# Products of constants between TensorE's working stretches, and the tokenizer's last normalisation handed over on the chip for two of sixteen pairs

## The chip, the cores and the metric

One core of one Trainium2 chip runs the whole program, a two-layer language-model tower. The metric is the device time of one execution in microseconds; the kernel before is timed three times, and one of its executions is profiled. TensorE is called PE here, VectorE DVE, ScalarE ACT, GpSimd POOL, and SyncE, which only issues DMAs, SP.

## What is computed

The input is 32 sequences of 512 token numbers. Cut to what matters (each `_layernorm` subtracts the mean over the 64 channels and divides by the deviation):

```
h = tok(x)                       # spectrum features, 64 -> 128 -> gelu -> 64
h = h + neighbourhood_attention(_layernorm(h))   # 8 heads, 31 neighbours, step 2
h = h + top2_of_8_experts(_layernorm(h))         # gelu experts
h = h + decayed_linear_attention(_layernorm(h))  # 0.99 ** distance
h = h + soft_experts(_layernorm(h))   # router softmax(mean over the batch), 8 experts,
                                      # three matrix products each
```

The result is 32 x 512 x 64, float32.

## The kernel before, in words

Two sequences form a pair: their 2 x 64 channels lie on the 128 partitions and the 512 positions in the free dimension. `s.h` holds the 16 pairs of the residual stream, `s.z` their normalised form and much scratch. Nearly all matrix products are float32 and show in the trace as two instructions each (passes).

The program is a row of seven blocks: `prepare`, `token_features`, `neighbourhood_attention`, `mixture_of_experts`, `decayed_attention`, `soft_router`, `soft_experts`. Each block gives every engine a program of its own; the engines meet at the end of each block, and none starts the next one before all have ended. Within a block, `unrolled(count, unroll, (lead, stage), ...)` writes out the loop: at each turn it runs the stages in the order listed, each `lead` items ahead. Every engine executes its instructions in order and waits on counting semaphores (`wait_ge`), so the list of stages is the order of work. `done(n)` is the count that says that item n is finished.

**Normalisation between blocks.** The means are folded into the weights. POOL squares each pair of `h` (`square`), PE sums the squares of four pairs at a time (`variance`, L494) into a bank in which the reciprocal deviations of the 32 sequences get 32 rows, and ACT turns the bank into `s.rstd` by a logarithm and an exponential. SP writes that to DRAM (`hop`, L500) and reads each row back broadcast over 64 partitions (`spread`, L512, two DMAs per pair) into one of four buffers `n_bc`; POOL multiplies (`scaled`, L522: `z = h * n_bc`). For the soft router the last four pairs do without DRAM: a product with the constant `near` spreads the deviations into a bank (L1868), and DVE multiplies (L1933).

**Tokenizer (`token_features`).** After eight variances of features (L697) ACT makes a reciprocal deviation, DVE splits it into two parts (L827, L829), and PE spreads it (L716). Then, for each step q of four sequences: `hidden` (L725, L728), GELU on ACT (L788, two banks `p_z`), `out_of` (L736), `tokens` on DVE (L839). At the end some weights are reflected (L761 to L768), and ACT makes the deviations for the attention (L791, L793).

**Neighbourhood attention.** For pair j: keys (PE L985, ACT L1120), queries (L992, L1113) and the values of each half of the positions (L1015, L1137) go through one bank `p_m` in turn; POOL multiplies the keys with four head masks (`keys_by_head`, L918); then, for each turn (even and odd positions), PE adds bf16 masks (L1051) and scores (L1057), DVE takes the maximum and subtracts (L1183, L1186), ACT exponentiates (L1143), PE transposes (L1066), ACT copies (L1150), PE applies the values (L1080).

**Experts.** The router's logits (L1335) are transposed (L1340) and go through some twenty small DVE operations; the expert matrices are L1364 (`first`), GELU L1425, `expand` L1376, DVE L1557, `second` L1392.

**Decayed attention, soft router, soft experts.** L1693 and L1698 project, L1708 scores; the soft router has sums (L1872), small products (L1888), transposes (L1892), a spreading over experts (L1897, L1900); the soft experts are three PE stages (L2003, L2013, L2025) with ReLU on ACT (L2050) and a DVE operation (L2070).

## Time and profile before

| | |
|---|---|
| time, median of three runs | 889.11 us (887.71 to 890.06) |
| the profiled execution's own time | 889.17 us |
| its span, mean granted clock | 887.4 us, 0.951 |
| busy: PE, DVE, ACT, POOL | 794.3, 577.1, 475.6, 304.3 us |
| first deviations for the attention ready, PE's last work in the tokenizer ends | 91.31, 90.90 us |
| first spread DMA issued, POOL's first multiply of the attention | 93.37, 97.05 us |
| POOL's and PE's first instruction of the decayed attention | 563.81, 565.21 us |
| spacing of the experts' GELU pairs from the third on | 1.9 us |

The page gives each engine's busy time and cuts the span into 40 slices with a line of the granted PE clock. Finer windows show where that clock changes. The timeline lists instructions in order: start in us, duration in us, engine, line, operation, output and inputs with their shapes, count, and in brackets how long the engine had been idle before and what released it. Neighbouring instructions of one line are merged (x2, x16, ...): the duration is then that of the group.

### The profile page before, as it was taken

How to read it: one execution, taken by the hardware profiler on the slowest of the kernel's cores; microseconds unless marked ns; L12 is line 12 of the kernel's file. 1: busy time of each engine (PE TensorE's matmuls, PEld its weight loads, DVE VectorE, ACT ScalarE, POOL GpSimd, SP SyncE). 2: the span in 40 equal slices, each digit the busy share in tenths (PEclk: the TensorE clock that was granted, in tenths of full speed). 3: DMA queues.
4: the chain of work that ended last, by engine and by line, in shares of the span. 5: the costliest groups of instructions: out<-in, count | busy, mean ns of one | idle time of the engine just before them, and what ended most of it. 6: DMA issues, size and time to landing. Idle time of an engine off the chain costs nothing. (4 is left out here: it accounts for less than half of the span.)

```text
span 887.4 us, 28760 instructions
## 1 busy us (share of the span) xinstructions
PE 794.3 (90%) x12566; PEld 405.7 (46%) x12566; DVE 577.1 (65%) x849; ACT 475.6 (54%) x656; POOL 304.3 (34%) x296
## 2 busy tenths in 40 slices
PE   4899499999999999669999889699997799999996
PEld 2222267677777776413333233376662233333332
DVE  5537167777776776546777865477773277777776
ACT  2244177778778777546566656422221355555553
POOL 3125535353364342212433554473543620000000
PEclk9979689999999999969999999999997699999999
DMA  4210411001001002010000220053321001111111
GB/s 105 26 30 1 126 31 45 10 5 59 8 4 53 15 5 63 3 60 1 1 2 2 72 73 1 13 168 105 87 90 31 13 25 49 48 49 49 48 49 36
DMA packets 38990, 36.83 MB, mean 42 GB/s; under 512 B 20881, under 2 KB 25138, under 8 KB 38738
## 3 DMA queue, kind: packets, MB, share of 16 engines
q1 hardware_dynamic: 37794, 33.04, 13.3%
q8 instruction: 100, 1.64, 0.8%
q10 hardware_dynamic: 1072, 1.95, 0.7%
q14 instruction: 24, 0.20, 0.1%
HBM read 19.24 MB, written 7.34 MB: 30 GB/s over the span
## 5 line engine op out<-in xcount | busy, mean ns | idle before, releaser
L2050 ACT ACTIVATE se_a<-se_p,cols 128x512 f32<-128x512 f32 x128 | 92.6, 773 | 76.2 <-PE se_p L2003 76.2
L1183 DVE TENSOR_REDUCE na_rowmax<-na_ps 128x16 f32<-128x1024 f32 x64 | 78.0, 1219 | 67.3 <-PE na_ps L1057 67.3
L2070 DVE SCALAR_TENSOR_TENSOR se_a<-se_p,cols,z 128x1024 f32<-128x1024 f32 x64 | 82.2, 1284 | 49.1 <-PE se_p L2013 49.1
L1425 ACT ACTIVATE z<-me_p,cols 128x512 f32<-128x512 f32 x128 | 81.0, 684 | 55.7 <-PE me_p L1364 51.0
L918 POOL TENSOR_TENSOR z<-na_k,const 128x512 f32<-128x512 f32 x64 | 64.5, 1040 | 128.4 <-ACT na_k L1120 128.4
L1557 DVE TENSOR_TENSOR me_gw<-me_pc,z 128x1024 f32<-128x1024 f32 x64 | 78.2, 1223 | 45.1 <-PE me_pc L1376 36.8
L487 POOL TENSOR_TENSOR n_sq<-h 128x512 f32<-128x512 f32 x64 | 68.3, 1072 | 94.1 <-DVE h L839 43.7
L1392 PE MATMUL me_py<-me_gw,w_out 64*64 64x512 f32 x512 | 88.1, 595 | 0.5 <-DVE me_gw L1557 0.5
L1364 PE MATMUL me_p<-z,moe_w 64*64 64x512 f32 x512 | 82.3, 617 | 5.8 <-ACT z L1425 5.8
L522 POOL TENSOR_TENSOR z<-h,n_bc 128x512 f32<-128x512 f32 x60 | 76.2, 1282 | 27.9 <-DMA n_bc<-n_spread 27.9
L1186 DVE TENSOR_TENSOR z<-na_ps,na_rowmax 128x1024 f32<-128x1024 f32 x64 | 78.3, 1224 | 2.2
L1066 PE MATMUL na_pt<-const,z 128*128 128x128 f32 x512 | 69.8, 280 | 2.5 <-ACT na_et L1150 1.7
L2003 PE MATMUL se_p<-z,f_w 64*64 64x512 f32 x512 | 69.7, 611 | 2.7 <-ACTq L535 1.8
L2013 PE MATMUL se_p<-se_a,f_w 64*64 64x512 f32 x512 | 68.0, 597 | 1.3 <-DVE se_a L2070 1.3
L1150 ACT ACTIVATE na_et<-na_pt 128x1024 f32<-128x1024 f32 x64 | 65.4, 1022 | 6.8 <-PE na_pt L1066 6.0
L1143 ACT ACTIVATE z<-z 128x1024 f32<-128x1024 f32 x64 | 67.4, 1053 | 1.6 <-DVE z L1186 1.1
L2025 PE MATMUL se_py<-se_a,w_out 64*64 64x512 f32 x512 | 67.5, 590 | 0.5 <-DVE se_a L2070 0.5
L1066 PEld LDWEIGHTS na_pt<-const,z 128*128 128x128 f32 x512 | 56.9, 142 | 18.2 <-issue 16.2
L1289 POOL TENSOR_TENSOR h<-h,me_even 128x512 f32<-128x512 f32 x15 | 20.1, 1339 | 99.7 <-DVE me_even L1572 99.7
L1137 ACT ACTIVATE na_v<-na_pm 64x512 f32<-64x512 f32 x64 | 38.5, 602 | 27.4 <-PE na_pm L1015 27.1
L1057 PE MATMUL na_ps<-z,na_q 32*32 32x256 f32 x2048 | 52.9, 397 | 0.1
L1080 PEld LDWEIGHTS na_po<-na_v,na_et 128*32 128x32 f32 x4096 | 41.4, 110 | 20.2 <-ACT na_et L1150 11.9
(300 smaller groups left out, 1266.7 us busy)
## 6 DMA issues: line engine op xcount, KB each, us to landing
n_bc<-n_spread SPq DMA_DIRECT2D x120, 128.0 KB, 3.0
z<-z SPq DMA_DIRECT2D x64, 128.0 KB, 2.4
out<-se_rows SPq DMA_DIRECT2D x16, 256.0 KB, 2.1
n_spread<-n_rstd SPq DMA_DIRECT2D x12, 256.0 KB, 2.0
const<-in_const ACTq DMA_DIRECT2D x1, 1050.0 KB, 7.0
const<-in_const ACTq DMA_DIRECT2D x1, 562.0 KB, 4.0
f_w<-in_L_ffn_W SPq DMA_DIRECT2D x4, 128.0 KB
const<-in_const ACTq DMA_DIRECT2D x1, 258.0 KB, 3.1
```

What stands on the lines that cost most here:

```text
L487: return nc.gpsimd.tensor_tensor(s.sq[p % 8][:], row(s.h, p), row(s.h, p), ALU.mult)
L522: return eng.tensor_tensor(row(s.z, p), row(s.h, p), s.bc[p % 4][:], ALU.mult)
L1066: mm = nc.tensor.transpose(p_t[:, c, :], e[b][:, 2 * c:2 * c + 2, :].rearrange("p h w -> p (h w)"), const(s, "ident"))
L1183: nc.vector.tensor_reduce(rowmax[b][:], scored, AX, ALU.max).then_inc(s_max, 1)
L1186: nc.vector.tensor_tensor(e[b], scored, rowmax[b][:].unsqueeze(2).broadcast_to([128, GROUPS, WIN]), ALU.subtract).then_inc(s_diff, 1)
L1364: mm = nc.tensor.matmul(hidden(at.n, b)[half[e2], :], s.moe_w1[half[b], 2 * ep + e2, :], row(s.z, at.of(4))[half[b], :], start=True, stop= ...
L1392: mm = nc.tensor.matmul(p_y[half[b], e2, :], s.moe_w2[half[e2], ep, :], gw[at.k % 2][half[e2], b, :], start=(ep == 0 and b != e2), stop=(e ...
L1425: nc.scalar.activation(g[at.n % 7][:, b, :], hidden(at.n, b)[:], ACT.Gelu, bias=col(s, "moe_b1", ep)).then_inc(s_g, 1)
L1557: nc.vector.tensor_tensor(gw[at.k % 2][:], p_c[:], g[at.n % 7], ALU.mult).then_inc(s_gw, 1)
L2003: mm = nc.tensor.matmul(hidden(at.n, e2)[half[b], :], s.f1_w1[half[e2], 2 * ep + e2, :], z[half[e2], :], start=True, stop=True, skip_group ...
L2050: nc.scalar.activation(a1[at.k % 2][:, e2, :], hidden(at.n, e2)[:], ACT.Relu, scale=col(s, "f1_g1", 2 * ep + e2), bias=col(s, "f1_be1", 2 ...
L2070: nc.vector.scalar_tensor_tensor(out=a2[at.k % 2][:], in0=p_2[:], scalar=col(s, "f1_be2", ep), in1=s.f1_w[:, ep, :].unsqueeze(1).broadcast ...
```

## The change

`keep_warm` issues bf16 products of two constants, identity (128x128) by expert masks (128x512), into a PSUM bank that nobody reads before it is written anew. It is called at seven places: after the tokenizer's last feature variance (12 products, preceded by a wait for the constants on POOL's count `n_zero`), at the tokenizer's end (4), ahead of the attention's first scores (6), around the attention's last variance (5 and 4), in the experts after the first logits (2), after the first two expert steps (8 and 3) and after the last two (3 and 7), after the decayed attention's last variance (8), and in the soft router (3, 8, 4, 8).

The border of tokenizer and attention: `NEAR = 2` pairs are normalised from a bank, by `near_of` with a second constant `near_first` and a DVE multiply; pair 0 at the tokenizer's end, pair 1 in the attention. SP spreads from pair 2 on, and POOL multiplies from pair 2 on, waiting for the first two. POOL splits the keys of the first two pairs one stage earlier in its order, and of pair 0 only two of four heads; DVE makes the other two. Queries of pair 0 go to bank `p_t` (`p_first`) and no longer wait for the keys to leave `p_m`, and its first values are made before its first scores instead of after.

```diff
+def keep_warm(nc, s, bank, count):
+    for _ in range(count):
+        nc.tensor.matmul(bank, s.ident_b[:], s.pick[:, 0].rearrange("p e n -> p (e n)"), start=True, stop=True, skip_group_check=True)
+NEAR = 2
+def near_of(nc, s, p, bank):
+    rows = slice(32 * p, 32 * p + 32)
+    return nc.tensor.matmul(bank[:], const(s, "near_first")[rows, :], s.rstd[rows, 0, :], start=True, stop=True, skip_group_check=True)
# constants
+        near[:, 2 * LAST + b, b, :] = near_first[:, b, b, :] = 1.0
# count of DMAs after which a broadcast buffer is ready
-    return 32 * (NP // 4 * stage + p // 4 + 1)
+    return 32 * (NP // 4 * stage + p // 4 + (p % 4 >= NEAR))
# token_features, PE after the last feature variance
+            te.wait_ge(s.n_zero, 10)
+            keep_warm(nc, s, p_z[0][:, 0, :], 12)
# token_features, PE at the end
+            te.wait_ge(s.n_rstd, quad(0, LAST))
+            near_of(nc, s, 0, p_m[0]).then_inc(s_near, 1)
+            keep_warm(nc, s, p_m[1][:], 4)
# token_features, DVE at the end
+            ve.wait_ge(s_near, 1)
+            v.tensor_tensor(row(s.z, 0), p_m[0][:], row(s.h, 0), ALU.mult).then_inc(s.n_z, 1)
# attention, POOL
-                for h in range(HL):
+                for h in range(HL if j > 0 else HL // 2):
                     for p in (2 * at.n, 2 * at.n + 1):
-                        pool.wait_ge(s.n_bc[p % 4], spread_done(0, p))
-                        scaled(nc.gpsimd, s, p).then_inc(s.n_z, 1)
+                        if p >= NEAR:
+                            if p == NEAR:
+                                pool.wait_ge(s.n_z, nth(0, NEAR - 1))
+                            pool.wait_ge(s.n_bc[p % 4], spread_done(0, p))
+                            scaled(nc.gpsimd, s, p).then_inc(s.n_z, 1)
-            unrolled(NP, 2, (5, before), (0, after), (4, keys_by_head), (0, derive))
+            unrolled(NP, 2, (5, before), (5, first_keys_by_head), (0, after), (4, next_keys_by_head), (0, derive))
# attention, SP
-            for p in range(NP):
+            for p in range(NEAR, NP):
# attention, PE: keys, queries, values and scores of the first pair
                     nc.tensor.matmul(p_m[:], s.a0_wqk[:, 1, :], row(s.z, j), start=True, stop=True).then_inc(s_k, 1)
+                    if j == 0:
+                        near_of(nc, s, 1, p_o).then_inc(s_near, 1)
+                    if j == 0:
+                        nc.tensor.matmul(p_first, s.a0_wqk[:, 0, :], row(s.z, j), start=True, stop=True).then_inc(s_q, 1)
+                        return
+                if at.n == 0:
+                    te.wait_ge(s_kd, done(0))
+                if at.n == 0:
+                    keep_warm(nc, s, p_t[:, 4:8, :].rearrange("p g c -> p (g c)"), 6)
+                    te.wait_ge(s_first, 1)
-            unrolled(TURNS, 2, (4, scores), (4, even_values), (6, queries),
+            unrolled(TURNS, 2, (4, scores), (4, even_values), (6, queries), (5, first_values),
...
+            keep_warm(nc, s, p_o[:], 5)
             variance_of(LAST)
+            keep_warm(nc, s, p_o[:], 4)
# attention, DVE ahead of its loop
+            ve.wait_ge(s_near, 1)
+            nc.vector.tensor_tensor(row(s.z, 1), p_o[:], row(s.h, 1), ALU.mult).then_inc(s.n_z, 1)
+            ve.wait_ge(s_kd, done(0))
+            for h in range(HL // 2, HL):
+                ins = nc.vector.tensor_tensor(kblk[0][:, h, :, :], kk[0][:], const(s, "headmask")[:, h:h + 1].unsqueeze(2).broadcast_to([128, 2, TG]), ALU.mult)
+            ins.then_inc(s_first, 1)
# experts, PE
+                    if c == 0:
+                        keep_warm(nc, s, p_c[:, 0, :], 2)
+                if at.n == 0:
+                    keep_warm(nc, s, p_c[:, 0, :], 8)
+                if at.n == 1:
+                    keep_warm(nc, s, p_c[:, 0, :], 3)
+                if at.n == EP * NP - 2:
+                    keep_warm(nc, s, p_r[:], 3)
+                if at.n == EP * NP - 1:
+                    keep_warm(nc, s, p_r[:], 7)
# decayed attention, PE after its last variance
+            keep_warm(nc, s, p_s[:, 0, :], 8)
# soft router, PE: after the sums, after the small products, after the transposes, at the end
+            keep_warm(nc, s, p_small[:], 3)
+            keep_warm(nc, s, p_shift[:], 8)
+            keep_warm(nc, s, p_small[:], 4)
+            keep_warm(nc, s, p_small[:], 8)
```

## Rows read from the trace of the kernel before

**Rows 1.** Windows of the six stretches at half clock: stretch, length, busy times, PEclk, DMA

```profile
39.94:53.59 13.65, 11.38 (x41) 3.69 (x42) 2.37 (x4) 4.60 (x4) 0.00 (x0) 0.50 0.29 49
94.55:118.45 23.90, 15.07 (x190) 7.80 (x190) 4.80 (x4) 6.29 (x8) 14.70 (x14) 0.50 0.36 111
377.86:394.93 17.07, 10.13 (x44) 2.06 (x44) 8.74 (x25) 6.38 (x10) 2.75 (x3) 0.50 0.23 78
565.60:569.01 3.41, 3.41 (x28) 2.15 (x22) 0.00 (x0) 1.26 (x2) 0.69 (x1) 0.50 0.24 57
671.41:681.65 10.24, 8.13 (x36) 1.77 (x40) 2.48 (x4) 2.60 (x3) 4.22 (x5) 0.50 0.23 53
688.48:702.13 13.65, 9.78 (x38) 3.05 (x42) 2.40 (x5) 3.98 (x7) 6.55 (x6) 0.50 0.00 1
sum 81.92, PE 57.90 PEld 20.52 DVE 20.79 ACT 25.12 POOL 28.92; mean PE 9.65 PEld 3.42 DVE 3.47 ACT 4.19 POOL 4.82
```

**Rows 2.** Timeline of the tokenizer from its last feature variance on

```profile
39.66 1.00 PE L716 MATMUL tf_pm<-tf_split,tf_own 64*128 64x512 f32 x2 [2.64 <-DVE tf_split L829]
...
41.18 2.09 PE L725 MATMUL tf_pz<-z,tok_w1s 32*128 32x512 f32 x8 [0.52 <-DVE z L834]
...
45.01 2.30 ACT L788 ACTIVATE z<-tf_pz,cols 128x1024 f32<-128x1024 f32 x2 [5.26 <-PE tf_pz L728]
...
54.65 1.14 PE L725 MATMUL tf_pz<-z,tok_w1s 32*128 32x512 f32 x8
...
56.69 2.30 ACT L788 ACTIVATE z<-tf_pz,cols 128x1024 f32<-128x1024 f32 x2 [3.12 <-PE tf_pz L728]
```

**Rows 3.** Timeline of the border of tokenizer and attention

```profile
98.36 2.08 PE L985 MATMUL na_pm<-z,w_in 128*128 128x512 f32 x2 [7.47 <-POOL z L522]
...
101.99 4.03 POOL L918 TENSOR_TENSOR z<-na_k,const 128x512 f32<-128x512 f32 x4
...
106.17 0.66 PE L1051 MATMUL na_ps<-winmask_b,ident_b 32*32 32x512 bf16 x16 [2.88 <-POOL z L918]
...
106.55 2.49 PE L1057 MATMUL na_ps<-z,na_q 32*32 32x256 f32 x64
...
116.39 2.33 PE L1057 MATMUL na_ps<-z,na_q 32*32 32x256 f32 x64
...
118.65 1.12 PE L992 MATMUL na_pm<-z,w_in 128*128 128x512 f32 x2
```

**Rows 4.** Timeline of one of the attention's last scores, at full clock

```profile
358.93 0.43 PE L1051 MATMUL na_ps<-winmask_b,ident_b 32*32 32x512 bf16 x16
...
359.16 1.55 PE L1057 MATMUL na_ps<-z,na_q 32*32 32x256 f32 x64
```

**Rows 5.** Timeline of DVE in the tokenizer's features

```profile
17.40 2.15 DVE L801 SCALAR_TENSOR_TENSOR z<-const,tok_phase,z 128x512 f32<-128x512 f32 x2 [2.54 <-ACT z L776]
...
20.18 0.74 DVE L801 SCALAR_TENSOR_TENSOR z<-const,tok_phase,z 128x512 f32<-128x512 f32 x1
```

**Rows 6.** Timeline of the change from attention to experts

```profile
377.21 1.36 PE L494 MATMUL na_ps<-n_sq,const 128*32 128x512 f32 x8 [1.96 <-POOL n_sq L487]
...
389.75 1.25 ACT L1425 ACTIVATE z<-me_p,cols 128x512 f32<-128x512 f32 x2
...
395.73 1.26 ACT L1425 ACTIVATE z<-me_p,cols 128x512 f32<-128x512 f32 x2 [0.74 <-PE me_p L1364]
```

**Rows 7.** Timeline from the decayed attention's last variance to the soft experts

```profile
671.57 1.94 PE L494 MATMUL da_py<-n_sq,const 128*32 128x512 f32 x8 [1.99 <-POOL n_sq L487]
...
675.46 2.09 PE L1868 MATMUL sr_pwide<-n_rstd,const 32*128 32x512 f32 x8 [1.96 <-PEq L1586]
...
690.79 2.09 PE L1897 MATMUL sr_pwide<-sr_by_expert,const 32*128 32x512 f32 x8 [0.69 <-ACT sr_by_expert L1912]
...
696.35 1.98 PE L2003 MATMUL se_p<-z,f_w 64*64 64x512 f32 x8 [1.78 <-ACTq L535]
...
702.66 1.28 DVE L2070 SCALAR_TENSOR_TENSOR se_a<-se_p,cols,z 128x1024 f32<-128x1024 f32 x1 [7.37 <-PE se_p L2013]
```

More of the change, by code:

```diff
@@ L58, in window_start @@
     return min(max(t * QT - KW // 2, 0), TG - WIN)
-CONST_PARTS = [("ident", 128), ("dft", 4 * 2 * NF), ("group", 4), ("block", 128), ("cos", T), ("sin", T), ("own", 32), ("place", 60), ("batch", NQ), ("house", 128), ("reflect", D), ("others", 38), ("kept", 1), ("near", 128), ("half_of", 38), ("mean128", 128),
+CONST_PARTS = [("ident", 128), ("dft", 4 * 2 * NF), ("group", 4), ("block", 128), ("cos", T), ("sin", T), ("own", 32), ("place", 60), ("batch", NQ), ("house", 128), ("reflect", D), ("others", 38), ("kept", 1), ("near", 128), ("near_first", 128), ("half_of", 38), ("mean128", 128),
                ("decay", 128), ("chunk_q", 128), ("chunk_k", 1), ("winmask", 4 * WIN), ("headmask", HL), ("vmask", 18), ("rank", NE), ("route_mean", NE),
@@ L82, in constants @@
     c["kept"] = (np.arange(128)[:, None] % D > 0) * 1.0
-    near = np.zeros((4, 32, 2, D))
+    near, near_first = np.zeros((4, 32, 2, D)), np.zeros((4, 32, 2, D))
     for b in range(2):
-        near[:, 2 * LAST + b, b, :] = 1.0
-    c["near"] = near.reshape(128, 128)
+        near[:, 2 * LAST + b, b, :] = near_first[:, b, b, :] = 1.0
+    c["near"], c["near_first"] = near.reshape(128, 128), near_first.reshape(128, 128)
     c["half_of"] = np.zeros((128, 38))
@@ L636, in token_features @@
             "s_part", "s_feat", "q", "s_prod", "var", "s_offset", "ln", "s_rstd", "s_split", "s_own", "s_rows", "x", "turned", "fetched")]
+        s_near = sem("s_near")
         s_m, s_moved, s_z, s_g = [sem(x) for x in ("m", "moved", "z", "s_g")]
@@ L906, in neighbourhood_attention @@
             sem(x) for x in ("q", "qd", "k", "kd", "blk", "v", "vd", "score", "max", "diff", "e", "et", "etd", "o", "rden", "on", "ot", "otd", "out", "h", "derived")]
+        s_first, s_near = sem("s_first"), sem("near")
+        p_first = p_t[:, 0:4, :].rearrange("p g c -> p (g c)")
         block = ctx.enter_context(nc.Block())
@@ L955, in derive, with first_keys_by_head, next_keys_by_head @@
                     derive_shared(nc, s, step, at.n - 6)
-            unrolled(NP, 2, (5, before), (0, after), (4, keys_by_head), (0, derive))
+            def first_keys_by_head(at):
+                if at.n < 2:
+                    keys_by_head(at)
+            def next_keys_by_head(at):
+                if at.n >= 2:
+                    keys_by_head(at)
+            unrolled(NP, 2, (5, before), (5, first_keys_by_head), (0, after), (4, next_keys_by_head), (0, derive))
         @block.sync
@@ L992, in queries, with first_values @@
                     nc.tensor.matmul(p_m[:], s.a0_wqk[:, 0, :], row(s.z, j), start=True, stop=True).then_inc(s_q, 1)
+            def first_values(at):
+                if at.n == 0:
+                    window_values(at)
             def even_values(at):
-                if at.k == 0:
+                if at.k == 0 and at.n > 0:
                     window_values(at)
@@ L1004, in window_values @@
                 te.wait_ge(s_vd, done(at.n - 1))
-                if par == 0:
+                if at.n == 0:
+                    te.wait_ge(s_kd, done(0))
+                elif par == 0:
                     te.wait_ge(s_qd, done(j))
@@ L1112, in fetch_queries @@
                     sc.wait_ge(s_score, done(2 * j - 3))
-                    nc.scalar.activation(q[j % 2][:], p_m[:].rearrange("p (t two) -> p two t", two=2), ACT.Identity, bias=col(s, "a0_bq")).then_inc(s_qd, 1)
+                    made = p_m[:] if j > 0 else p_first
+                    nc.scalar.activation(q[j % 2][:], made.rearrange("p (t two) -> p two t", two=2), ACT.Identity, bias=col(s, "a0_bq")).then_inc(s_qd, 1)
             def fetch_keys(at):
@@ L1120, in fetch_keys, with fetch_first_values @@
                     nc.scalar.activation(kk[j % 2][:], p_m[:].rearrange("p (t two) -> p two t", two=2), ACT.Identity, bias=col(s, "a0_bk")).then_inc(s_kd, 1)
+            def fetch_first_values(at):
+                if at.n == 0:
+                    fetch_values(at)
             def fetch_even_values(at):
-                if at.k == 0:
+                if at.k == 0 and at.n > 0:
                     fetch_values(at)
@@ L1366, in first @@
                 mm.then_inc(s_w1, 1)
+                if at.n == 0:
+                    keep_warm(nc, s, p_c[:, 0, :], 8)
+                if at.n == 1:
+                    keep_warm(nc, s, p_c[:, 0, :], 3)
             def expand(at):
```

2 lines of the change are left out of this document (1 added, 1 removed).

## The prediction

> **What bounds the kernel now.** I read the page first: PE is busy in nearly every slice, and its line of granted clock is below full in a few of them. So I cut the span into narrow windows and noted where the clock changes. It stands at its lower level (0.50, that is 1.2 of 2.4 GHz) in six stretches before the last microseconds, each around a change of block [rows 1]: 81.92 us together, of which PE is busy 57.90. The reader is to see that no stretch is idle throughout: if each busy microsecond halved and nothing else were waited for, 28.9 us would go. That is the ceiling of the clock's part. The timeline of each stretch then says how much of its PE work has somebody waiting behind it.
>
> What PE did before each fall: idle from 37.02 to 39.66, fell at 39.94 [rows 2]; idle from 90.90 until 98.36, fell at 94.55 [rows 1, 3]; before 377.86, 565.60, 671.41 and 688.48 it had likewise waited for the last variance, a block change or the small steps of the soft router. Before each rise it had been busy without a gap, or nearly.
>
> **What a product of constants costs.** No instruction of before has its form (bf16, 128x512, all 128 rows). The nearest are the masks, bf16 with 512 columns, sixteen at once in separate parts of the array: 0.66 us at half clock [rows 3], 0.43 at full [rows 4]. The difference, 0.23, is the streaming at full clock, so I price one in a row of many at 0.22 us at full and 0.44 at half. Bounds: 0.43 each if nothing overlaps, 0.2 if only the streaming counts. At 0.22 the twelve of the tokenizer take 2.6 us: exactly the hole of 2.64. The others are 4, 6, 5+4, 2+8+3, 3+7, 8, and 3+8+4+8 (0.7 to 1.8 us each group).
>
> **Tokenizer (gain 4.5, if the clock holds).** Hidden layers run from 41.18 to the GELU at 45.01, 3.83 us; the same step at full clock is 54.65 to 56.69, 2.04 [rows 2]. GELU of step 0 comes 1.8 earlier. Step 1 waits for it, takes 2.0 instead of 3.8 (3.6 earlier now), and step 2, which today waits until 54.65 for PE's backlog, would start when the GELU of step 1 ends: 41.2 + 2.0 + 2.4 + 2.0 + 2.4 = 50.1. That is 4.5 us. After it GELU (2.30 per pair) sets the pace, unchanged.
>
> **Border of tokenizer and attention (gain 10.5, if it holds).** Today the deviations end at 91.3, go through DRAM and come back broadcast; POOL multiplies pairs 0 to 3 before it may split keys; PE reaches the keys at 98.36 after idling 7.47, POOL's four key parts take 101.99 to 106.02, and the scores end at 109.04 [rows 3]. After: `near_of` (two passes, about 1.0) to 92.4, a DVE multiply (0.7, as L834's half of the pair after 40.3) to 93.1, block change, first PE instruction 94.2 (taken halfway between an immediate start and the 1.4 us that the decayed attention's block needs). Then in PE's order: keys 1.1 (as L992 at full [rows 3]), `near_of` 1.0, queries 1.0, values 1.0, six products 1.3: 99.5. Beside it: keys fetched 96.1, two key parts on POOL at 1.0 (half of 4.03 [rows 3]) to 98.2; on DVE, row 1 then two parts at 0.7 to 98.4. PE sets it. Scores at full take 0.2 + 1.55 [rows 4], so they end at 101.3, 7.7 earlier. The second scores then wait for DVE's maxima (4.9 behind the first) and take 1.8: end 108.2 against 116.39 + 2.33 = 118.72 [rows 3]: 10.5. The second pair's key parts (POOL, 103.7 to 107.8) come 11 us earlier too, so nothing waits there. POOL's multiplies for pairs 2 and 3 start after the first split and need transfers that are in by 97 to 98.5; SP's queue loses four DMAs. What is late next is DVE's maximum after the first scores, with PE idle 2.5 us.
>
> A rule that speaks against splitting the keys over two engines: two DVE multiplies of that stretch with both inputs in SBUF take 2.15 beside a POOL multiply, where one beside a memset takes 0.74 [rows 5]. The Trainium skill ("SBUF — State Buffer", section "Who interferes with whom") has such a DVE operation and a GpSimd operation that reads SBUF exclude each other; the trace agrees, with these 2.15 and 0.74. By it the four parts run one by one, which puts the end of the four parts near 99.6 instead of 98.4, 0.1 behind PE, and takes 0.1 from the sum.
>
> **Attention to experts (2.8).** The last variance (1.36, 0.65 of it after the fall) gains 0.3 [rows 6]. Logits and transposes before the router's DVE chain gain 0.9 + 0.45, so the first GELU pair moves from 389.75 to 388.4. From it to the third pair today 5.98 [rows 6]; at full I count 4.8 (two GELU steps of 1.9 and one set of logits, 1.0): 1.2 more. The products after the first two expert steps lie in PE's wait for GELU. Less sure: PE is still idle from about 379.2 to 381.6, and if the clock falls in that wait the gain is 1.5, since the eleven products bring it back before the third pair.
>
> **Experts to decayed attention (1.7).** The whole stretch, 3.41 us, is PE-busy [rows 1] with DVE waiting behind: half. Three products between the last two steps fit a gap of 0.5 almost (0.1 lost).
>
> **Decayed attention to soft router (2.4 to 3.7).** The eight products stand behind the variance (L494, 671.57), not before it, so the fall at 671.41 is untouched [rows 7]. At half clock they need 3.5 us from 673.5, rising on the way: PE ends at 675.9 and holds the block's end 0.8 longer. Then everything from 675.46 to 681.65 is PE-bound at half clock and runs at full, 3.1 saved: 2.4 net. Where the fall does not come before the variance, 3.7. I take 2.9.
>
> **Soft router to soft experts (3.2).** Transposes gain 0.45, four products behind them take 0.2 back, expert rows 2.09 to 1.1 and the shift the same: but then eight products (1.8) replace DVE's 0.7 as the block's last work. Net 1.0. From 696.35 to DVE's first operation at 702.66 there are 6.31 us [rows 7], three PE groups of 2.0 at half: 4.0 at full. 2.3 more.
>
> **Sum.** 4.5 + 10.5 + 2.8 + 1.7 + 2.9 + 3.2 = 25.6 with the clock up wherever its gap is filled. But waits of 1.9 to 2.6 us remain in three places: tokenizer (between the first spread and step 1), the first softmax, and the change to the experts. What rows show is that the clock fell behind a wait of 2.64 and again amid the router's short waits, at 688.48, so I expect it to fall at one or two of the three, for about as long as the shortest stretch of rows 1, costing 1.5 to 1.7 each at the first two and 1.3 at the third: about 3.5 in expectation. 25.6 - 3.5 = 22.1. The profiled execution is 889.17 us (span 887.4), the median of three 889.11: no difference to carry. Forecast 889.1 - 22.1 = 867.0.
>
> The Trainium skill ("TensorE: Matmul & The Clock Gate", Part 1, "What's actually happening") calls the gate's observation free-running: it does not restart with the kernel, so where it turns differs between executions. No run here shows that yet; by it falls at those three places come in some executions and not in others, and the median would still lie between 863.5 and 869.
>
> **Rivals.**
> - *The clock holds everywhere* (25.6): 863.5. For: PE would be idle nowhere longer than 2.6 us. Against: 2.64 at 37 us was enough today.
> - *It falls at all three waits, and the router's steps (small weights, 8 columns) do not hold it either*: 25.6 - 4.5 - 2.5 = 18.6, so 870.5. For: the clock fell at 688.48 after PE had worked through just those steps, and waits of about 2 us stay between them where a group of products ends early.
> - *Little but the border works*: the products do not hold the clock; fewer transfers and the earlier values give 2.8, and first scores still end near 108.1. With products partly in the way: 884 to 886.
> - *Slower*: the same, with the products at half clock (0.44 each) in front of waiting work. Eight behind the last variance hold the block 2.0, seven behind the experts 1.6, the router's 8+4+8 hold its chain 1.4 + 1.1 + 2.7, two and eight at the experts' start 1.0: 9.8 - 2.8 = 7.0 slower, 896. It decides if fewer than about 7 us of the six stretches' clock loss come back. Against: every rise today followed PE work of the same or a thinner kind.
>
> **How the numbers follow.** Forecast (one or two falls) 0.50, own range 864.5 to 869.5; holds everywhere 0.18; falls at all 0.22; little 0.06; slower 0.04. For 8 in 10 the range takes the first three with the product's price bounds: 861.5 to 873.5. Within 0.3% is 2.7 us, about what a measurement tells from nothing: faster 0.94, same 0.02, slower 0.04.
>
> **What would show it.** The granted clock full from 37 us through the hidden layers; first scores ending 12 us earlier in absolute time; first block instructions of PE after 94; variance before the soft router still at half clock and PE the last to finish that block; twelve products in 2.6 us. Wrong if: products last 0.4 us at full clock, PE's first instruction of a block waits for them, or the first softmax's wait grows.

## The result, and the profile after

The changed kernel takes 878.57 us (median of 4, 872.67 to 879.30), the kernel before on the same chip 889.59 us (median of 4): ratio 0.986, 95% interval 0.981 to 0.991. That is 11.0 us faster, half of the 22.1 forecast, and outside the range (861.5 to 873.5). Timed once more on another chip (run g1, below) it gave 0.9854 (0.9828 to 0.9881), 14.0 us by the medians. The profiled execution took 878.94 us, with a span of 877.1.

First the windows of the changed kernel in which PEclk, the granted clock of TensorE (PE), stands at 0.50, as [rows 1] showed them for before:

```profile
core 0: us, PE busy (x) PEld busy (x) DVE busy (x) ACT busy (x) POOL busy (x), PEclk, DMA share, GB/s
46.88:50.30 3.42, 3.42 (x14) 0.77 (x8) 0.06 (x1) 2.00 (x2) 0.00 (x0) 0.51 0.22 47
91.31:101.55 10.24, 9.60 (x27) 3.71 (x28) 3.03 (x3) 3.55 (x7) 5.38 (x4) 0.50 0.42 130
108.28:111.70 3.42, 3.35 (x84) 1.66 (x82) 0.46 (x2) 1.97 (x2) 3.42 (x4) 0.50 0.00 0
374.56:377.97 3.41, 3.30 (x13) 1.02 (x14) 0.00 (x0) 1.02 (x2) 0.09 (x1) 0.50 0.33 94
384.79:388.20 3.41, 3.41 (x14) 0.56 (x17) 2.95 (x10) 1.64 (x3) 0.00 (x0) 0.50 0.00 0
569.11:572.50 3.39, 3.31 (x22) 2.96 (x22) 0.00 (x0) 0.00 (x0) 0.00 (x0) 0.50 0.42 159
688.58:692.00 3.42, 3.42 (x20) 0.98 (x16) 0.25 (x1) 1.74 (x3) 3.42 (x4) 0.50 0.00 0
sum 30.71, PE 29.80 PEld 11.67 DVE 6.75 ACT 11.91 POOL 12.31; mean PE 4.26 PEld 1.67 DVE 0.96 ACT 1.70 POOL 1.76
```

30.7 us at half clock instead of 81.9: that part of the change works. But PE is busy in nearly all of what is left, so each remaining fall costs about half its length. Three of the places were expected (46.88, 108.28, 374.56 to 388.20), three were not: the change of blocks at 91.31, the first outputs of the decayed attention at 569.11, and the first steps of the soft experts at 688.58, for which the sum had the full clock.

The timeline of the border, answering to [rows 3]:

```profile
88.21 1.12 PE L530 MATMUL tf_pm<-n_rstd,const 32*128 32x512 f32 x2 [0.47 <-ACT n_rstd L812]
89.49 0.81 PE L502 MATMUL tf_pm<-pick_b,ident_b 128*128 128x512 bf16 x3 [0.16 <-issue]
91.95 2.05 PE L1019 MATMUL na_pm<-z,w_in 128*128 128x512 f32 x2 [1.65 <-ACTq L548]
93.93 2.07 PE L530 MATMUL na_po<-n_rstd,const 32*128 32x512 f32 x2
95.93 2.08 PE L1027 MATMUL na_pt<-z,w_in 128*128 128x512 f32 x2
96.64 2.42 DVE L1237 TENSOR_TENSOR z<-na_k,const 128x512 f32<-128x512 f32 x2
97.93 1.98 PE L1060 MATMUL na_pm<-w_in,z 128*64 128x128 f32 x16
99.84 2.25 PE L502 MATMUL na_pt<-pick_b,ident_b 128*128 128x512 bf16 x6
102.25 1.55 PE L1105 MATMUL na_ps<-z,na_q 32*32 32x256 f32 x64
107.46 1.23 PE L1114 MATMUL na_pt<-const,z 128*128 128x128 f32 x8 [2.61 <-ACT z L1198]
109.16 2.47 PE L1105 MATMUL na_ps<-z,na_q 32*32 32x256 f32 x64
```

The hole of 7.47 us in front of the keys is gone, as forecast. In its place stand one of 1.65 (no instruction of PE's is to be had there: the blocks change), in which the clock falls, and four steps of 2.0 where 1.0 to 1.1 was counted. The six products take 2.25 at half clock, in front of scores whose inputs are ready by 99.1. The first scores end at 103.80 (before 109.04), the second at 111.63 (118.72).

The timeline of the later places, answering to [rows 6, 7]:

```profile
384.73 1.02 PE L502 MATMUL me_pc<-pick_b,ident_b 128*128 128x512 bf16 x2 [0.16 <-issue]
385.68 1.94 PE L1396 MATMUL me_pr<-z,w_in 128*32 128x512 f32 x8
389.00 1.27 ACT L1496 ACTIVATE z<-me_p,cols 128x512 f32<-128x512 f32 x2 [0.72 <-PE me_p L1427]
569.19 1.98 PE L1798 MATMUL da_py<-da_sm,da_v 128*64 128x128 f32 x16 [2.65 <-ACT n_rstd L1835]
...
669.40 1.14 PE L1940 MATMUL sr_pwide<-n_rstd,const 32*128 32x512 f32 x8 [0.99 <-PEq L1657]
681.38 1.14 PE L1972 MATMUL sr_pwide<-sr_by_expert,const 32*128 32x512 f32 x8
686.27 1.09 PE L2079 MATMUL se_p<-z,f_w 64*64 64x512 f32 x8 [1.08 <-ACTq L548]
691.75 1.28 DVE L2146 SCALAR_TENSOR_TENSOR se_a<-se_p,cols,z 128x1024 f32<-128x1024 f32 x1 [7.27 <-PE se_p L2089]
703.98 1.78 DVE L2160 TENSOR_TENSOR se_res<-se_res,se_odd 128x512 f32<-128x512 f32 x1
```

The soft router runs at full clock: its spreads are 11.98 us apart, where [rows 7] has 15.33. The decayed attention's outputs run at half clock behind a wait of 2.65 us; that wait was there before the change too, but the clock held over it. In the trace of before:

```profile
576.79 1.09 PE L1727 MATMUL da_py<-da_sm,da_v 128*64 128x128 f32 x16 [2.66 <-ACT n_rstd L1763]
```

### The profile page after: what moved, and what is told of

Same layout as the page of the kernel before. It is cut to its first block and busy times, and to the rows that moved or that the text cites. A ratio compares the mean times of both kernels' runs of the same rounds, so it can differ in the third digit from the quotient of the medians.

```text
span 877.1 us, 28927 instructions
## 1 busy us (share of the span) xinstructions
PE 802.1 (91%) x12648; PEld 409.7 (47%) x12655; DVE 581.8 (66%) x853; ACT 476.1 (54%) x656; POOL 300.8 (34%) x292
## 3 DMA queue, kind: packets, MB, share of 16 engines
q8 instruction: 101, 1.65, 0.8%
## 5 line engine op out<-in xcount | busy, mean ns | idle before, releaser
L941 POOL TENSOR_TENSOR z<-na_k,const 128x512 f32<-128x512 f32 x62 | 62.5, 1039 | 136.8 <-ACT na_k L1171 136.8
L1427 PE MATMUL me_p<-z,moe_w 64*64 64x512 f32 x512 | 80.4, 602 | 5.0 <-ACT z L1496 5.0
L1128 PEld LDWEIGHTS na_po<-na_v,na_et 128*32 128x32 f32 x4096 | 41.5, 110 | 20.1 <-ACT na_et L1205 11.4
```

The source lines that it names most:

```text
L1427: mm = nc.tensor.matmul(hidden(at.n, b)[half[e2], :], s.moe_w1[half[b], 2 * ep + e2, :], row(s.z, at.of(4))[half[b], :], start=True, stop= ...
```

## The experiments

All times are medians, with the ratio to the kernel before run beside it. "Stretches" are pieces of 3.4 us at half clock, the length of the shortest in [rows 1], counted until the last microseconds of the kernel. A "fall" is a change of the granted clock from full to half; a clock that is "held" does not fall.

**Splitting the change.** e1 turns all products off (`for _ in range(0)` in `keep_warm`). e2 is the kernel before with the products alone, but for the four and the six at the border. e3 and e4 change the border only:

```diff
 e3
+            keep_warm(nc, s, p_m[1][:], 2)
             te.wait_ge(s.n_rstd, quad(0, LAST))
             near_of(nc, s, 0, p_m[0]).then_inc(s_near, 1)
-            keep_warm(nc, s, p_m[1][:], 4)
+            keep_warm(nc, s, p_m[1][:], 8)
 e4
                 if at.n == 0:
-                    keep_warm(nc, s, p_t[:, 4:8, :].rearrange("p g c -> p (g c)"), 6)
                     te.wait_ge(s_first, 1)
```

> The changed kernel with no products of constants at all: the border without transfers is the whole change. Theory 'falls' (the waits that are left still drop the clock, and what lies between them runs at half of it): the border keeps its own gain of about 4 us, because the six products that stood in front of the first scores (2.25 us at half clock) are gone but the scores then run at half clock (about 2 us more); all other gains (tokenizer 3, router and change to its experts 5) go back: about 885.5 us, 883.5 to 887.5. Rival 'order' (the new border is limited by its own chain of keys, spread, queries and values and by the products it queues): without products the border alone gives 6 us or more, 883 or less. Rival 'products carry nothing': 879, as with them.

> The kernel before with all the products of the change but the four at the end of the tokenizer and the six before the first scores, and with its old border by transfers. Theory 'falls': gain 11 minus the border's 4, so about 882.5 us (881 to 884.5), and 885.5 + 882.5 together make the whole change. Rival 'order' (the border gives most): 885 or more.

> The changed kernel with two products before near's first spread in the tokenizer and eight after it instead of four: TensorE has no idle time from 88 us to 91 us. Theory 'falls': the clock stays full at the change of blocks, keys, spread, queries and values take about 1.1 us each instead of 2, the six products 1.3 instead of 2.25: the first scores end 3.5 to 5 us earlier against the end of the tokenizer, less up to 0.9 us by which the block ends later: 875.5 us (874 to 877). Rival 'order': the same as the changed kernel or slower (878.5 to 879.5), because the chain waits for kblk's heads on GpSimd and VectorE, whose times the clock does not touch.

> The changed kernel without the six products that TensorE queues before the first scores. Theory 'falls': they cost 2.25 us in front of scores whose inputs were ready at 99.1 us, but they raise the clock for the scores and what follows; without them the scores start about 2 us earlier and take about 2 us longer: within 1 us of the changed kernel (877.5 to 879.5). Rival 'order' (the queued products are the loss): 876.5 or less.

Measured beside 887.48 for before: e1 883.47 (0.9958, 0.9938 to 0.9977), e2 880.10 (0.9916, 0.9890 to 0.9941), e3 874.58 (0.9865, 0.9832 to 0.9898), e4 873.58 (0.9845, 0.9820 to 0.9870). The border alone gives 4.0 us, the products alone 7.4, together 11.4: the two parts add up to the change, and each is what "falls" had (4 and 7). Both times lie 2 us under those expected because those were reckoned from 889.6 us for before, which takes 887.48 on this chip. e3 and e4 have ratios within the interval of the changed kernel's (g1, below): for e4 that is what was expected, for e3 it is not, since "falls" had 3 us there. In e3's trace the block change held its clock, and the clock fell in the first softmax for twice as long instead:

```profile
91.55 1.10 PE L1020 MATMUL na_pm<-z,w_in 128*128 128x512 f32 x2 [1.65 <-ACTq L548]
97.34 1.55 PE L1106 MATMUL na_ps<-z,na_q 32*32 32x256 f32 x64
102.56 1.97 PE L1115 MATMUL na_pt<-const,z 128*128 128x128 f32 x8 [2.61 <-ACT z L1199]
104.86 2.48 PE L1106 MATMUL na_ps<-z,na_q 32*32 32x256 f32 x64
```

**The changed kernel again, and the waits that it left open.** g1 is the changed kernel itself. g2 puts products into four waits that the change left open or half filled (7 before the tokenizer's second hidden layer, 8 for 4 behind the attention's last variance, 16 for 8 behind the experts' first layer, 10 before the decayed attention's first outputs). g3 is e3 and e4 together with nine products in the first softmax. g4 is both. The two new lines of most weight:

```diff
                 if at.n == 0:
+                    keep_warm(nc, s, p_s[:, 0, :], 10)
                     te.wait_ge(s.n_rstd, quad(2, LAST))
...
                 def stage(at):
+                    if at.n == 0 and b == 0:
+                        keep_warm(nc, s, p_t[:, 4:8, :].rearrange("p g c -> p (g c)"), 9)
                     te.wait_ge(s_e, done(2 * at.n + b))
```

> The changed kernel once more, so that it stands on the same chip as the three that follow: 11 us less than the kernel before (ratio 0.987).

> The changed kernel, its border left as it is, with products in the four waits that it left open: 7 before the second hidden layer of the tokenizer (2.0 us idle), 8 instead of 4 behind the last variance of the attention, 16 instead of 8 behind the experts' first layer (2.4 us idle), and 10 before the first outputs of the decayed attention (2.6 us idle). Theory 'falls': the falls at 46.9, 374.6, 384.8 and 569.1 us go: 1.4 + 2.8 + 1.5 = 5.7 us faster than the changed kernel, less about 0.5 us for products that end late: 4 to 6 us faster. Rival 'elsewhere' (a fall moves to the next wait when one is held, and the products hold up waiting work): within 1.5 us of it.

> The changed kernel with the border held (two products before the first near spread of the tokenizer, eight after it), without the six products before the first scores, and with nine products in the first softmax (2.6 us idle). Theory 'falls': what holding gave (first scores 3.7 us earlier by their own) and what the six cost (2.6 us) add up, less the overlap of the two: second scores end 5 to 6 us earlier and the time is 4.5 to 6 us under the changed kernel. Rival 'order': with the clock held, what is left is the wait for kblk's heads on VectorE: 3 us or less.

> Both of the two before. Theory 'falls': the sum, 9 to 11 us under the changed kernel (about 866 us where it takes 876), with a mean granted clock over 0.99; that is what the prediction had forecast for the change itself. Rival 'elsewhere': the falls come back at other waits (the change to the soft router, the soft experts), and less than 7 us is left.

Measured beside 888.40: g1 874.42 (0.9854), g2 872.79 (0.9838, 0.9810 to 0.9865), g3 875.40 (0.9858, 0.9836 to 0.9880), g4 872.15 (0.9831, 0.9806 to 0.9856). "Falls" is refuted three times: against g1, g2 gives 1.6 us where 4 to 6 were expected, g3 is 1.0 us slower where 4.5 to 6 were, and g4 gives 2.3 where 9 to 11 were; none of the three is told from nothing by these intervals. So "falls" alone is not enough, although g4's trace has 2 stretches at half clock and a mean clock of 0.995. And g1's profiled execution has a span of 870.6, 6.5 us less than the first one of the very same program. Here is its border:

```profile
90.75 1.10 PE L1019 MATMUL na_pm<-z,w_in 128*128 128x512 f32 x2 [1.65 <-ACTq L548]
91.78 1.12 PE L530 MATMUL na_po<-n_rstd,const 32*128 32x512 f32 x2
...
94.91 1.47 PE L502 MATMUL na_pt<-pick_b,ident_b 128*128 128x512 bf16 x6
96.54 1.55 PE L1105 MATMUL na_ps<-z,na_q 32*32 32x256 f32 x64
103.82 2.12 PE L1105 MATMUL na_ps<-z,na_q 32*32 32x256 f32 x64
```

The same instructions behind the same wait of 1.65 us, and the clock stays up until the first softmax: the first scores end 5.7 us earlier than in the first trace, 1.2 of it from the tokenizer.

g4 shows three other things that eat what a held clock gives. Its eight products behind near's spread hold the block's end: keys start 4.69 us after the deviations (g1 3.79). Products stand in front of the experts' second logits. And in the attention PE stops inside runs of like matmuls, with no semaphore that it waits for ("issue"; what the stops are is shown further down):

```profile
113.21 0.88 PE L1063 MATMUL na_pm<-w_in,z 128*64 128x128 f32 x12
114.97 0.44 PE L1063 MATMUL na_pm<-w_in,z 128*64 128x128 f32 x4 [0.88 <-issue]
...
381.07 0.82 PE L502 MATMUL me_pc<-pick_b,ident_b 128*128 128x512 bf16 x3
381.82 1.06 PE L1400 MATMUL me_pr<-z,w_in 128*32 128x512 f32 x8
```

**Trims, the late products alone, and second traces.** h1 is g4 with 4 for 8 behind near's spread, 3 products before the first scores, none before the second logits, 1 for 3 and 5 for 7 at the experts' end, 4 for 8 behind the decayed attention and behind the router. h2 is the kernel before with the products from the decayed attention's last variance on. h3 is the kernel before, h4 is g4.

> g4 with fewer products where its trace shows them ending after the work that they stood beside: 4 instead of 8 behind near's spread, 3 before the first scores, none instead of 3 in front of the second logits, 1 instead of 3 before the experts' last second layer, 5 instead of 7 behind it, 4 instead of 8 behind the decayed attention's last variance and 4 instead of 8 behind the soft router. Theory now ('products in front of waiting work cost what they last'): 0.9 at the border, 0.4 at the second logits, 0.5 at the experts' end, 0.4 and 0.7 at the two block ends: 2.5 us under g4, about 869.5 us. Rival ('falls alone decide'): fewer products bring falls back, the same as g4 or slower.

> The kernel before with only the products behind the decayed attention's last variance and in the soft router. If the terms for these places hold as forecast (2.9 and 3.2), 6.1 us faster than before: ratio 0.993. If they are what the changed kernel's executions showed from the last variance on (3.0 and 1.2 to 1.9), 4.2 to 4.9 us: ratio 0.995.

> The kernel before once more, for its trace: if falls depend on how an execution lies against the clock's observation, some of the six half-clock stretches start elsewhere or are missing, although the program is the same; if they depend on the program alone, they stand where they stood.

> g4 once more, for a second trace. In its first one TensorE stood still inside runs of like matmuls of the attention for 3.9 us in all without any wait in the profile (0.7 us in g1's). If those belong to the program (more instructions ahead of the attention), they stand at the same places; if to the execution, elsewhere or not at all, and the span is up to 3 us shorter.

Measured beside 888.22: h1 872.52 (0.9823, 0.9802 to 0.9845), h2 882.73 (0.9932, 0.9920 to 0.9945), h4 871.31 (0.9796, 0.9774 to 0.9818), h3 one execution of 885.16 us. h2 answers to the forecast terms 2.9 + 3.2: 0.9932 is 6.0 us (5.5 by the medians). h1 was expected 2.5 us under g4 and is not. Its trims do what they were to do where they stand: the third GELU pair of the experts comes 17.06 us after the attention's last row (g4 18.33), the second scores 17.30 after the deviations (g4 18.24). But with 4 products for 8 the clock fell around the decayed attention's last variance and stayed down in the router (its start to its logits 9.28 us instead of 7.50): part of the rival. Why the median is g4's all the same is not shown: the execution traced (869.73 us, clock 0.991) is the fastest of the five, and the other four, with mean clocks of 0.983 to 0.987, have no trace.

```profile
375.68 1.09 PE L1432 MATMUL me_p<-z,moe_w 64*64 64x512 f32 x8 [0.77 <-ACT z L1499]
376.70 1.07 PE L1401 MATMUL me_pr<-z,w_in 128*32 128x512 f32 x8
```

These are h1's: with the three products gone the logits follow 1.0 us behind the start of the expert's layer, where g4 has 1.8.

h3 has 20 stretches where before's first trace has 24, around the same waits but begun and ended elsewhere (the tokenizer's is 3.4 us up in between, the border's 17.1 us long instead of 23.9). The second scores of h3 end 24.93 us after the deviations, 27.41 in [rows 3]'s trace.

**What PE's stops are.** h4 has 2.7 us of them in the attention, g4 3.8. Four of h4's six stand at the very instruction at which g4 has one, with another length. Two of them (before the last sixteen of a run of 64, and before the last mask of a run of sixteen), first g4's, then h4's:

```profile
119.10 0.32 PE L1132 MATMUL na_po<-na_v,na_et 128*32 128x18 f32 x16 [0.40 <-issue]
...
341.56 0.39 PE L1101 MATMUL na_ps<-winmask_b,ident_b 32*32 32x512 bf16 x1 [0.89 <-issue]
```

```profile
118.35 0.32 PE L1132 MATMUL na_po<-na_v,na_et 128*32 128x18 f32 x16 [0.95 <-issue]
...
338.77 0.38 PE L1101 MATMUL na_ps<-winmask_b,ident_b 32*32 32x512 bf16 x1 [0.46 <-issue]
```

Over all 20 traces the attention, from the second scores to its last row, has 67 stops of more than 0.15 us. Counted in PE's weight loads from the start of the program they stand at 963, 1215, 3735, 5626, 5878, 7642 and so on, whatever the instruction there: all 67 are multiples of 126 apart, give or take two. And each of them ends 1.20 to 1.58 us after a packet of 16 KB of the DMA queue 8, of kind "instruction" (about 100 such packets in a kernel), has landed; only about a tenth of the attention lies at that distance behind a packet. So the reading is that PE stands where a new packet of its own instructions begins, when that packet comes late: the place is the program's, the length the execution's (the one program of PE that g1 and j1 share has 0 to 2.6 us of stops in its six traces). It fits every stop, but no experiment changed the packets. The five traces without products at the border (before, h3, e1, e2, h2) have 0 to 0.8 us of stops, the fifteen with them 0 (j1) to 4.0 (i3), 2.1 on average; whether the change moved the packets' edges to worse places is not shown.

**Three more traces of the changed kernel, and the trims with the eight kept.**

> The changed kernel, for a third trace. Theory 'falls come by execution': the time lies on one line with the falls, about 1.3 us for each half-clock stretch of 3.4 us, between 870.6 us of span at four of them and 877.1 at nine. Rival: the same falls as in one of the two and another time, so that something else sets it.

> The changed kernel, for a fourth trace; what each theory expects is as for the third: a span on the line of 1.3 us for each half-clock stretch, or off it.

> h1 with the eight products behind the decayed attention's last variance kept. Theory: the router keeps its clock (sums to logits in 7.5 us instead of 9.3) and the trims at the border, the second logits, the experts' end and the router's end stay: 1 to 2 us under h1, about 870.5 to 871.5 us, ratio 0.980. Rival 'falls alone decide': 872.5, ratio 0.982 or more.

> The changed kernel, for a fifth trace; what each theory expects is as for the third: a span on the line of 1.3 us for each half-clock stretch, or off it.

i1, i2 and i4 took 876.72, 877.65 and 877.06 us, spans 874.9, 875.9, 875.3, with 6, 6 and 7 stretches. The line of 1.3 us for each stretch gives 873.2, 873.2 and 874.5: right in its direction, 0.8 to 2.7 us low. What is over it is a start 0.4 to 0.7 us later than in g1 and PE's stops in the attention (2.4, 2.6 and 1.7 us, g1 0.6). i3 872.19 beside 888.70 (0.9822, 0.9787 to 0.9857): the router held (7.50), but with four products behind near's spread the clock fell right behind the block change (second scores 20.41 after the deviations). The 1 to 2 us expected did not come; the number is the rival's. In the two traces each set of trims lost at one place part of what it gave at others, but h1 has the same four products and its border held.

Over all the traces: with four products behind near's spread the clock fell within 1.8 us of the keys' start in 8 of 11 (in the first one and e4 before the keys, in i1 to i4, j1 and j2 behind their start; not in g1, g2, h1), with eight in one of four (g3, at 94.5; not in e3, g4, h4). That is a hint and no proof that eight hold it better.

**Where the soft experts lose it.** j1 is the changed kernel, j2 is i3, both with GpSimd's sixteen additions of the soft experts' block split:

```diff
             for p in range(NP):
+                if p == 8:
+                    pool.wait_ge(s_res, done(0))
                 nc.gpsimd.tensor_tensor(row(s.h, p), row(s.h, p), s.f1_r, ALU.add).then_inc(s_shifted, 1)
```

> The changed kernel, in which GpSimd makes eight of its sixteen additions (1.23 us each), then waits until VectorE has made its first addition of the residual, then makes the other eight. Theory 'two engines on one port': that VectorE addition takes 0.69 us instead of 1.6 to 3.3, the eight later GpSimd additions end before pair 1's, and the time from logits to the end falls from 200.3 us to 199.2 with a fall in the soft experts' first steps (the usual case) and to 197.7 without: 1.1 to 2.6 us faster than the changed kernel, ratio to before 0.9835. Rival 'clock only': 200.3 us as before, ratio 0.985 to 0.986.

> The trimmed version that keeps the eight (i3), with the same split. Theory: its VectorE addition of 3.27 us falls to 0.69, and 2.6 us go where no fall follows: 1.5 to 2.6 us under i3, ratio 0.980. Rival 'clock only': 0.982 as i3.

Measured beside 888.58: j1 873.99 (0.9853, 0.9831 to 0.9875), j2 871.64 (0.9803, 0.9781 to 0.9825). First g1, then j1, the first addition of the residual on VectorE and what GpSimd does:

```profile
678.91 19.74 POOL L2065 TENSOR_TENSOR h<-h,z 128x512 f32<-128x512 f32 x16 [15.59 <-POOLq L1905]
683.67 1.28 DVE L2146 SCALAR_TENSOR_TENSOR se_a<-se_p,cols,z 128x1024 f32<-128x1024 f32 x1 [5.76 <-PE se_p L2089]
695.90 3.29 DVE L2160 TENSOR_TENSOR se_res<-se_res,se_odd 128x512 f32<-128x512 f32 x1
```

```profile
680.06 9.86 POOL L2067 TENSOR_TENSOR h<-h,z 128x512 f32<-128x512 f32 x8 [15.59 <-POOLq L1905]
686.40 1.28 DVE L2148 SCALAR_TENSOR_TENSOR se_a<-se_p,cols,z 128x1024 f32<-128x1024 f32 x1 [7.34 <-PE se_p L2091]
698.62 0.69 DVE L2162 TENSOR_TENSOR se_res<-se_res,se_odd 128x512 f32<-128x512 f32 x1
699.40 9.89 POOL L2067 TENSOR_TENSOR h<-h,z 128x512 f32<-128x512 f32 x8 [9.48 <-DVE se_res L2162]
710.02 0.69 DVE L2162 TENSOR_TENSOR se_res<-se_res,se_odd 128x512 f32<-128x512 f32 x1
```

In g1 the addition ends at 699.19, 0.54 us after GpSimd's sixteen; with those out of its way it takes 0.69. In 16 of the 18 traces with the undivided row of sixteen the addition ends 0.55 us behind the last of them, whatever its own length (0.93 to 3.29 us); in the other two (e1, h3) it comes later and takes 0.69. That much is shown. The gain is not: from logits to the end j1 takes 200.12 us, the five traces of the changed kernel 200.21 to 200.35. In j1's execution the clock fell at 683.1, the first VectorE product came 6.34 us after GpSimd's start (g1 4.76), and PE set the pace again: the second addition of the residual is 29.96 us behind GpSimd's start, against 30.11 in both the first trace and g1. For an execution with such a fall 1.1 us were expected, and they did not come either. What the split is worth where the clock holds there was not seen, and j2's ratio beside i3's (0.9803 and 0.9822) lies within both intervals.

## Why the prediction was half right

The kernel before, twice, and the changed kernel in its five executions, cut at the same instructions (us from each mark to the next; the last two columns are what the change gave on the mean of the five, against the first trace of before and against h3):

| stretch | before | h3 | first | g1 | i1 | i2 | i4 | forecast | gave | against h3 |
|---|---|---|---|---|---|---|---|---|---|---|
| start to first hidden layer | 41.18 | 41.78 | 41.16 | 41.38 | 41.75 | 42.11 | 41.81 | 0 | -0.5 | 0.1 |
| to the deviations | 50.13 | 48.55 | 47.00 | 45.58 | 45.59 | 45.59 | 45.58 | 4.5 | 4.3 | 2.7 |
| to the end of the second scores | 27.41 | 24.93 | 23.48 | 18.98 | 22.24 | 22.19 | 22.25 | 10.5 | 5.6 | 3.1 |
| to the attention's last row | 256.57 | 255.54 | 256.89 | 256.61 | 257.67 | 258.33 | 256.91 | 0 | -0.7 | -1.7 |
| to the experts' third GELU | 20.44 | 20.41 | 20.47 | 18.35 | 19.43 | 19.48 | 18.31 | 2.8 | 1.2 | 1.2 |
| to the decayed attention's start | 169.51 | 169.50 | 170.17 | 171.67 | 170.16 | 170.16 | 171.55 | 0 | -1.2 | -1.2 |
| to its first outputs | 11.55 | 11.45 | 10.02 | 10.03 | 10.03 | 10.02 | 10.02 | 1.7 | 1.5 | 1.4 |
| to the router's start | 98.67 | 98.66 | 100.21 | 100.23 | 100.25 | 100.18 | 101.03 | 0 | -1.7 | -1.7 |
| to the router's logits | 10.49 | 10.19 | 7.49 | 7.50 | 7.49 | 7.50 | 7.49 | 2.9 | 3.0 | 2.7 |
| to the end | 201.45 | 202.39 | 200.21 | 200.27 | 200.29 | 200.34 | 200.35 | 3.2 | 1.2 | 2.1 |
| span | 887.4 | 883.4 | 877.1 | 870.6 | 874.9 | 875.9 | 875.3 | 25.6 - 3.5 | 12.6 | 8.6 |

Two executions of before differ by 4.0 us, most of it in the tokenizer and at the border, so what a stage gave is known to no better than about 2.5 us there.

**Right.** The price of a product: eight take 1.90 us and four 1.04, so 0.22 for each further one, and two at half clock 1.02, which fits 0.44 each beside the same rest of 0.14. The tokenizer: 4.5 us against the first trace of before where the clock holds over the wait of 2.04 (four of five), 3.1 where it falls; 3.0 and 1.6 against h3. The start of the decayed attention 1.5, the soft router 3.0 to the logits. The sum for a border at full clock: 16.9 us forecast from the deviations to the second scores, 17.30 measured (h1, with three products for the six and nine in the first softmax), so 10.1 of the 10.5. The first VectorE product of the soft experts 4.0 us behind PE's first, as in g1. Between executions the falls do move: the Trainium skill ("TensorE: Matmul & The Clock Gate", Part 1, "What's actually happening") has it that the observation runs freely, and here one program had 4 to 9 stretches at half clock and spans from 870.6 to 877.1.

**The step that failed** is in the sum: "25.6 with the clock up wherever its gap is filled", less falls at three named waits and at none besides, so that a fall anywhere else was put at nothing. The three waits themselves did about what was counted for them: the clock fell in the tokenizer in one trace of five (1.4 us), in the first softmax in five (1.1) and at the change to the experts in three (1.6), 2.3 us on the mean where 3.5 was allowed. (The 3.5 does not follow from "one or two of the three" at 1.3 to 1.7 each, which is 1.3 to 3.4.) Of the 13.0 us that the mean of the five lacks against 25.6, nearly 11 lie elsewhere, in places that were filled or overlooked:

- *Border, 10.5 forecast, 5.6 given (3.1 against h3).* I counted the block change as a short pause. From the deviations to the keys there are 3.79 us where I had 2.9, 1.65 of them with PE idle, and the clock fell there in four executions of five (3.2 to 4.5 us: in the first trace keys, spread, queries, values and the six products run at half clock, in the others what comes behind the keys). In the first softmax it fell in all five, 1.1 us. The six products are themselves part of the loss: from the deviations to the first scores' end e4 takes 14.14 us, the first trace 15.64, both with a fall at the block change.
- *Decayed attention, 0 forecast, -1.7 given.* Its first outputs stand behind a wait of 2.65 us. The clock fell there in all five (1.55 us), where it held in both traces of before; why it held there these traces do not tell (in j1 and h2 it held too). It is not the products elsewhere that bring this fall: e1, which has none, has it as well. Of the 14 traces without products in this wait 10 fell, of the six with ten products none. The waits were in the trace of before, and I listed only those inside the half-clock stretches of [rows 1]. With ten products in it the stretch takes 98.67 us (g2, h1), as before the change, or 99.6 (g4, h4, i3, j2), where the clock falls at the stretch's end instead. In g4's timeline the outputs take 1.09 us instead of 1.98:

```profile
561.66 2.10 PE L502 MATMUL da_ps<-pick_b,ident_b 128*128 128x512 bf16 x9 [0.16 <-issue]
564.06 1.09 PE L1803 MATMUL da_py<-da_sm,da_v 128*64 128x128 f32 x16 [0.30 <-ACT n_rstd L1840]
```

- *Experts, 2.8 forecast, 0.0 left at their end.* The third GELU comes 2.1 us earlier at best, and 3.4 with eight products behind the attention's last variance and none in front of the second logits (h1, i3: 17.06); 0.75 of it is the three products, which stand between the first and the third GELU pair (4.65 us in g2, 3.90 in h1). Behind it the stretch is at least 0.65 us longer than before in every trace of the change, for which the sum had 0.1. 0.28 of it are the products at its end (e2 has 0.29 more than before; 1 and 5 for 3 and 7 take 0.3 back in h1 and i3), and 0.36 stand in e1 too, which has no products at all. In g1 and i4 the clock also fell at 498 and 502 us, in the midst of the experts, 1.4 to 1.5 us more.

**Too large by itself:** the soft experts' 2.3. Two effects take turns. Mostly (four of five) the clock falls in their first steps; where it holds (g1), VectorE's addition ends only 0.54 us behind GpSimd's sixteen and the 1.5 us are gone too. I had the rule in hand ([rows 5] and "SBUF — State Buffer", section "Who interferes with whom", of the Trainium skill) and applied it to the keys alone. There it holds too: the two VectorE parts of the keys take 2.15 to 2.42 us beside GpSimd. About 0.9 us of the 2.0 missing is in the baseline: h3 needs 202.39 to the end, and h2 against its neighbours gives 6.0 us by ratio and 5.5 by the medians for the last two terms.

**The rivals.** "Falls at all three waits, and the router's steps do not hold" had 870.5: its first half was the case in the first trace, its second was not. None had a fall behind the block change once products stood before it, nor falls at waits outside the six stretches of [rows 1], nor time lost by PE's stops. The first comparison lies 5.1 us above the range, and g1 0.9. "Slower" and "little but the border works" are out: the products alone give 7.4 us in e2.

**What is left open.** Holding more waits does not add up: g4 and h4 have 2 and 3 stretches left and a gain over the changed kernel of 2.3 us beside g1, and 0.6% by ratio in h4. Traces show the later block end, products before waiting work and PE's stops in the attention (up to 4.0 us); no experiment takes these apart. What decides in one execution where the clock falls stays open too. The best ratios are h4's 0.9796 and j2's 0.9803; that either beats the changed kernel's 0.9854 by more than 0.3% is not shown: g4, the same program as h4, gave 0.9831.

## What to carry to other kernels

To price a change that lifts a clock, list every wait of PE in the kernel that is as long as those before its falls, those at full clock today too: with the clock up everywhere, each of them can be the next fall, and which of them is differs between executions of one program. So take two or three traces of the kernel before, not one, and fill a wait only to just short of its end, never in front of a step whose input may already be there. An engine that is made to start earlier can lengthen what another does at that moment: look at the two together. And where PE stops with no semaphore to wait for, count its instructions up to the stop and look at when the packets of its instruction queue land before putting the stop down to chance.

## What the runs showed of the hardware

- One program, five profiled executions: 4, 6, 6, 7 and 9 stretches of 3.4 us at half clock, spans 870.6 to 877.1 us; and 20 and 24 for the kernel before, 883.4 and 887.4.
- At a block change with 1.65 us of PE idle the clock fell within 1.8 us of the next matmul's start in 8 of 11 traces with four products before it, and in 1 of 4 with eight.
- Behind a wait of 2.6 us in the decayed attention the clock fell in 10 of 14 traces, and in none of six with ten products in the wait.
- An addition on VectorE with both inputs in SBUF took 3.29 us beside a row of GpSimd additions and ended 0.54 us after their last; 0.69 us without them.
- PE stood still for 0.2 to 1.4 us with no semaphore to wait for, 0 to 4.0 us in all in one attention: always at counts of its weight loads that are multiples of 126 apart (give or take two), and always until 1.20 to 1.58 us after a packet of 16 KB of the "instruction" DMA queue 8 had landed (67 stops of 67, in 20 traces).
